# Rotary attention in a six-block decoder: query and content-key projections issued together as paired 64-row matmuls

## What is computed

```python
def _L1_attn_ref(x, W_DQ, W_UQ, W_QR, W_DKV, W_UK, W_UV, W_KR, W_O):
    # D_MODEL 256, N_HEADS 16, D_H 16, D_HR 8, D_LATENT 64; x is the layer-normed stream
    c_q = x @ W_DQ                                        # 64 wide
    Qc = (c_q @ W_UQ) per head;  Qr = rope((c_q @ W_QR) per head)
    c_kv = x @ W_DKV                                      # 64 wide
    Kc = (c_kv @ W_UK) per head; Kr = rope(x @ W_KR), the same for all heads
    V = (c_kv @ W_UV) per head
    scores = clip(concat(Qc, Qr) . concat(Kc, Kr), -80, 80), causal
    weights = softmax(scores / sqrt(24))
    return (weights @ V) @ W_O
x = x + _L1_attn_ref(_layernorm(x), ...)
```

## Time and profile before

| | us |
|---|---|
| median of three runs | 3155.16 |
| lowest, highest | 3151.1, 3158.64 |
| span of the profiled execution | 3229.4 |
| the rotary stage in it, first to last instruction | about 1461.7 to 1735 |
| PE busy in the whole span | 2825.7 (87%) |
| DVE busy | 2269.1 (70%) |
| ACT busy | 1656.0 (51%) |

### The profile page before, as it was taken

One profiled execution on the slowest core, in us unless ns is written; L12 is line 12 of the kernel. 1 busy time (PEld: TensorE's weight loads), 2 busy tenths in 40 slices (PEclk: granted clock), 3 DMA queues, 4 the chain that ended last, 5 costly groups with the idle time before them and its releaser, 6 DMA issues. The chain is left out here.

```text
span 3229.4 us, 75851 instructions
## 1 busy us (share of the span) xinstructions
PE 2825.7 (87%) x28240; PEld 2055.9 (64%) x28240; DVE 2269.1 (70%) x4822; ACT 1656.0 (51%) x3243; POOL 957.9 (30%) x1219
## 2 busy tenths in 40 slices
PE   7998999999999997758997899999997999955880
PEld 6887566666666665547885566666665777745770
DVE  5998567777777775557886677767754999863446
ACT  4776555555655554334553344444444878742330
POOL 0000344555554554440001000000001145445661
PEclk9999999999999998789998899999997999977995
DMA  7930345544555453361000333333314778765557
GB/s 176 292 91 0 113 148 154 159 139 138 162 163 146 138 154 110 115 193 31 0 0 20 65 74 71 72 65 73 73 37 119 219 227 235 219 183 166 171 166 249
DMA packets 364787, 413.71 MB, mean 128 GB/s; under 512 B 108016, under 2 KB 330512, under 8 KB 364368
## 3 DMA queue, kind: packets, MB, share of 16 engines
q1 hardware_dynamic: 218176, 220.63, 25.7%
q10 hardware_dynamic: 127216, 139.94, 15.3%
q0 software_dynamic: 19104, 49.22, 4.5%
HBM read 125.33 MB, written 252.45 MB: 117 GB/s over the span
## 5 line engine op out<-in xcount | busy, mean ns | idle before, releaser
L814 POOL TENSOR_TENSOR x_rstd<-x_var,g_minus_half 112x1 f32<-112x1 f32 x128 | 74.6, 583 | 710.7 <-DVE x_var L810 710.1
L2194 DVE TENSOR_REDUCE x_top<-x_scores 112x2 f32<-112x750 f32 x256 | 228.3, 933 | 81.2 <-PE x_scores L2036 78.7
L1369 ACT ACTIVATE x_probs<-x_held,x_minus_top 112x488 f32<-112x488 f32 x256 | 177.7, 697 | 173.6 <-DVE x_minus_top L1425 173.6
L1242 POOL TENSOR_TENSOR x_probs<-x_probs,x_inverse 112x488 f32<-112x488 f32 x256 | 250.4, 998 | 10.2
L1283 PE MATMUL x_ring<-w_xkv,x_kv 128*122 128x512 f32 x512 | 236.3, 594 | 0.0
L1276 PE MATMUL x_ring<-x_kv,w_xkv 128*128 128x488 f32 x512 | 232.0, 586 | 1.1 <-ACT x_kv L1345 1.1
L932 ACT ACTIVATE x_v<-x_ring 122x512 f32<-122x512 f32 (+1 forms) x224 | 113.0, 505 | 182.9 <-PE x_ring L1283 152.0
L2141 ACT ACTIVATE x_probsT<-x_scores 125x1792 f32<-125x1792 f32 x96 | 159.7, 1664 | 83.3 <-PE x_scores L2056 83.3
L1419 DVE SCALAR_TENSOR_TENSOR x_held<-x_scores,x_keep 112x976 f32<-112x976 f32 x128 | 150.4, 1175 | 73.2 <-PE x_scores L1296 50.8
L814 POOL TENSOR_TENSOR a_rstd<-a_var,g_minus_half 112x1 f32<-112x1 f32 x64 | 35.6, 556 | 537.7 <-DVE a_var L810 537.7
L3102 POOL DMA_INDIRECT expert_replies<-m_rows,m_reply_of x143 | 140.6, 983 | 94.7 <-ACT m_rows L3212 62.3
(11 more groups left out here) (471 smaller groups left out, 7442.7 us busy)
## 6 DMA issues: line engine op xcount, KB each, us to landing
expert_slots<-d_empty ACTq DMA_DIRECT2D x32, 3612.0 KB, 17.3
by_position<-r_by_position SPq DMA_DIRECT2D x64, 784.0 KB
first_slots<-d_empty SPq DMA_DIRECT2D x8, 3612.0 KB, 33.9
r_bias<-by_position SPq DMA_DIRECT2D x64, 392.0 KB
m_rows<-expert_slots SPq DMA_DIRECT2D x143, 129.0 KB
x_kq_swapped<-x_kq_raw ACTq DMA_DIRECT2D x64, 243.5 KB, 3.5
x_slots<-x_kq SPq DMA_DIRECT2D x512, 30.4 KB
m_rows<-expert_replies SPq DMA_DIRECT2D x32, 448.0 KB, 8.5
```

The lines of the kernel that those rows point to most:

```text
L1242: self.nc.gpsimd.tensor_tensor(probs, probs, self.inverse[0:T, u:u + 1].to_broadcast([T, XK]), ALU.mult).then_inc(self.weighted, 1)
L1369: nc.scalar.activation(self.probs[u % 6][0:T, :], self.held[m % 2][0:T, i, :], ACT.Exp, scale=self.scale, bias=self.minus_top[0:T, m % 2, ...
L2194: nc.vector.tensor_reduce(self.top[0:T, g, 2 * half:2 * half + 2], self.scores[0:T, at:at + 1024].rearrange("t (a c) -> t a c", c=512)[:, ...
```

## The change

The steps `q` and `kc` become one piece of PE work. At the place of `q`, PE claims both banks, waits for `a_c`, and then issues eight matmuls in alternation: for each of the four groups one on rows 0 to 63 (`aq` with c_q) and one on rows 64 to 127 (`akc` with c_kv). The halves that were multiplied by zero weights are left out. `kc` keeps its place in the plan for the ring and for DVE, but PE does nothing there. In the plan `q` moves ahead of `turnk`, to right behind `scores`; `kc` moves to behind `scale`, so that DVE makes `a_k` ahead of `bound`; `onT` moves behind `kc`.

```diff
-        self.plan = Flow(4, [("stats", 0), ("scores", 2), ("turnk", 1), ("onT", 4), ("scale", 0), ("q", 1), ("heads", 3),
-                             ("bound", 2), ("kc", 1), ("xT", 0), ("turnq", 1), ("v", 1), ("c", 0), ("kr", 0), ("exp", 2),
+        self.plan = Flow(4, [("stats", 0), ("scores", 2), ("q", 1), ("turnk", 1), ("scale", 0), ("kc", 1), ("onT", 4), ("heads", 3),
+                             ("bound", 2), ("xT", 0), ("turnq", 1), ("v", 1), ("c", 0), ("kr", 0), ("exp", 2),
                              ("project", 4), ("back", 3)])
...
-        elif name in ("q", "kc"):
-            bank = ring.claim(pe, c, body)
-            if name == "q":
-                self.ready(pe, "c", b)
+        elif name == "q":
+
+            spots = {"q": c, "kc": self.plan.order.index("kc")}
+            banks = {n: ring.claim(pe, spot, body) for n, spot in spots.items()}
+            self.ready(pe, "c", b)
             for g in range(HG):
-                ins = nc.tensor.matmul(bank[:, g * T:(g + 1) * T], W["a" + name][:, g * P:(g + 1) * P], self.c[:, :],
-                                       start=True, stop=True)
-            ring.filled(ins, c)
+                for n, rows in (("q", slice(0, 64)), ("kc", slice(64, P))):
+                    ins = nc.tensor.matmul(banks[n][:, g * T:(g + 1) * T], W["a" + n][rows, g * P:(g + 1) * P], self.c[rows, :],
+                                           start=True, stop=True)
+                    if g == HG - 1:
+                        ring.filled(ins, spots[n])
```

## The result

| | before | changed |
|---|---|---|
| median of six runs, us | 3157.85 (3151.1 to 3159.71) | 3181.2 (3167.2 to 3187.24) |
| ratio to before, 95% interval | | 1.0071 (1.0056 to 1.0085) |
| span of the profiled execution, us | 3229.4 | 3180.0 |
| this stage in it, from its first `stats` (808) to the next stage's, us | 1458.66 to 1742.42: 283.8 | 1436.45 to 1746.27: 309.8 |
| frames 4 to 31: start of `a_q_turned`, first to last, us | 1493.2 to 1720.0: 8.40 a frame | 1473.6 to 1723.4: 9.25 a frame |

The account below looks back on a forecast made before the run. A closed chain through PE and DVE was taken to bound the kernel; 18.2 us for 28 full frames plus 2.9 for the end frames gave +21.1, 3155.2 to 3176.3 us, range 3163 to 3200 (own range 3168 to 3187).

Parts of the forecast that it names:

- Which engine bounds the stage: Steady frames: a closed chain through PE and DVE (a_q_turned, project, back, scores, turnk) sets 8.40 us a frame.
- The place: Pair between scores and turnk delays turnk; a full frame grows by X - 0.33 = 0.65 us, to 9.05.
- X: The pair's own time on PE ahead of turnk: 0.88 us plus 0.10 for the pass to full array, 0.98 us.
- slack: Time turnk could come later before DVE's a_kr_plain waits: 0.23 and 0.14 us, mean 0.19 us.
- The wait before a_xn: DVE's wait for the norm's power on POOL, 0.18 us a frame, would give back 0.14 us.
- Their sum: Full frame longer by X - 0.19 - 0.14 = 0.65 us; 18.2 us over 28 frames.
- The frames at the ends: Frames 2, 3 and 32, where DVE already waits for turnk, lose 0.98 us each, 2.9 us; frame 1 loses 0.
- signs of being wrong: Pair under 0.6 or over 1.3 us, a_kr_plain not waiting, project not waiting for a_q_turned, or clock not 1.00.
- PE as the bound: PE's issue time sets each of 32 frames, so its saved time gives -31 us, 3124; chance 0.08.
- The halves not pairing: The 64-row halves of q and kc do not run side by side: X = 1.96, 3206.7 us; chance 0.06.
- X at 0.44: The pair runs at the pace of 32-row tiles: 3159.6 us, no change that shows; chance 0.06.
- The clock falling: PE's clock drops to 0.82 with more idle time: another 21 us over 28 frames, 3197.6 us; chance 0.06.

Follow-up runs that it names:

- run with `turnk` first: Changed kernel with turnk put ahead of the paired q and kc in the plan, against the kernel before: 3156.3 us, ratio 0.9996.
- old order: Paired matmuls with the whole plan of the kernel before, the pair at the place of q, against the kernel before: 3158.47 us, ratio 1.0009.
- freed bank: Changed kernel with turnk ahead of the pair and v ahead of turnq, giving project v's bank, against the kernel before: 3137.0 us, ratio 0.9934.
- line of three kernels: Against the kernel before: changed with half of the pairs behind turnk, 1.0038; changed, 1.0071; changed with full 128-row matmuls, 1.0172.

## Why the prediction was right, point by point

- **Which engine bounds the stage.** Right: a chain closed through both, not PE's 99%. It rests on one reading, that `project` was released by `a_q_turned` with PE's loads idle. The run with `turnk` first shows it directly: PE's loads idle 0.84 us a frame ahead of `project` and nothing is gained (ratio 0.9996). The old order agrees (1.0009), and the freed bank shows the other link, 8.35 to 7.61 us a frame.
- **The place.** Right, and its form too (frame longer by X less the slack): the line of three kernels has slope one. The slack was 0.22 us, 0.19 forecast.
- **X.** Mis-sized: 0.98 forecast, 1.08 measured. The eight pairs take 0.88 us as forecast. The term that was too small is the pass from the pair to the full array: `turnk` loads 1505.53 - 1505.23 = 0.30 us after the last pair where the pace is 0.11, so the pass costs 0.19 or 0.20 us, and 0.10 was forecast. That 0.10 was read in the kernel before from the end of the last load of `scores` to `turnk`. But the loads overlap, and from start to start it is 0.28 us, in the kernel before to `turnk` (1605.24 to 1605.52) and in the changed one to the first pair (1504.17 to 1504.45):

```profile
1504.17 0.17 PEld L1809 LDWEIGHTS a_scores<-a_q,a_k 32*112 32x112 f32 x1
```

  So the way out of `scores` costs the same as before, 0.98 us from its first load, and adds nothing to X; one pass is new, as forecast, with twice its price. By the Trainium skill's rule (TensorEngine Tiling, "Key Properties" under "Tiling Modes": a change of tiling mode drains TensorE) there is a gap at each change of tiling, and the trace agrees with that. The prediction's 1.08 by that rule, a second gap of 0.10, is the measured number by luck.
- **The wait before a_xn.** Wrong by its step "the norm's power on POOL coming late": 0.14 us a frame was to come back and did not. In the changed kernel POOL is done at 1505.30 + 0.55 = 1505.85, DVE's `a_kr_turned` at 1506.66 + 0.28 = 1506.94, and `a_xn` still starts 0.24 us later. In the loop's frames the gap is 0.24 and 0.13 us by turns, 0.18 in the mean, in all nine kernels measured, whatever their order. In frame 2, ahead of the loop, `a_xn` follows after 0.03 us (1452.89 + 0.28 to 1453.20). The trace shows what stands in the gap: register instructions of DVE's own sequencer, which aren't counted as busy. Line 818, where DVE waits for the norm's power ahead of `a_xn`, has one in each of the 28 frames of the loop, and in frames 1 to 3 a plain semaphore wait in its place (DVEq is the sequencer):

```profile
L818 DVEq ALU_OP  x28: 40/40/40, 1470.1 to 1719.9; - x28
```

```profile
L818 DVEq EVENT_SEMAPHORE  x3: 50/50/50, 1444.5 to 1461.2; - x3
```

  In the frame shown it runs at 1507.1, behind another one at 1507.0, both after the end of `a_kr_turned` and ahead of `a_xn` at 1507.17. No run was made without them.
- **Their sum.** +0.85 us a frame instead of +0.65: 0.10 from X, 0.14 from `a_xn`, less 0.03 of slack. Over the 27 frames from the first `a_q_turned` to the last that is 23 us; with the 2.7 and 0.4 us of the next point it makes up the 26.1.
- **The frames at the ends.** Up to `a_q_turned` of frame 4 the stage lost 2.7 us (from the first `stats`: 1493.15 - 1458.66 = 34.5 before, 1473.59 - 1436.45 = 37.1 now). The forecast for this stretch was 2 x 0.98 for frames 2 and 3 and 0.65 for frame 4, 2.6 in all, and that it came out is luck: up to `a_q_turned` of frame 1 it was 0.55 us shorter, and then frames 2, 3 and 4 were 1.72, 0.52 and 0.97 us longer. At the end +1 us was forecast and +0.4 measured (last `a_q_turned` of frame 31 to the next stage, 22.4 and 22.8). Frame 32 did wait 1.75 us for `turnk` where it had waited 0.67, but it grew by only 0.6 us, and the drained frames behind it were 0.2 shorter.
- **The total.** Stage +26.1 in the profile, +22.4 by the ratio of the runs, +21.1 forecast. The range holds them all. The two errors have the same sign and show on the profile's stage, 5 us more than forecast; that the runs came within 1.3 us of the forecast is partly the luck of their spread.
- **What the profile would show.** `a_kr_plain` waits 0.86 us a frame; the prediction's list said 0.5 to 0.7, although its own sum (0.98 less 0.19) gave 0.79. 0.66 before `g_residual` came, 0.97 before `project` came nearly (over a microsecond was forecast). The frame of 9.05 and the end of the wait before `a_xn` did not come. None of the signs of being wrong did.
- **The rivals.** PE as the bound: refuted. The halves not pairing: loads 0.01 us apart, refuted. X at 0.44: 1.08. The clock falling: granted 1.00 in all windows of the stage from 1452 on, with the idle times of 0.3 to 1.0 us in each frame. In the start it did fall once: full in 1444 to 1446, where PE was busy 0.54 of the 2 us, half (0.50) in 1447 to 1449 and full again from 1450. The kernel before had half clock up to 1469, in its frame 1, and full clock from then on. So part of frame 1 ran faster than before and part of frame 2 slower. Only one execution of each kernel is profiled, so whether this belongs to the change isn't shown.

## What to carry to other kernels

When two engines are both nearly always busy, find who released whom at each hand-over and close the loop; time saved outside that loop buys nothing as long as the loop is what sets the pace, and work moved into it costs its full length beyond the slack, which can be read to a tenth of a microsecond before the change. A step that the other engine waits for should be issued ahead of bulk work that nobody waits for yet. In a ring of banks the position in the plan is also a dependency: here a change of two entries that gave `project` another bank, together with the paired matmuls behind `turnk`, made the kernel 0.66% faster where neither alone showed a gain in the runs.

## What the runs showed of the hardware that was not expected

Passes between tilings show in the spacing of the weight loads, best from start to start, since the loads overlap. From the last load of `scores` (32-row tiles) it is 0.28 us to the next step, and the same whether that is the 64-row pair (1504.17 to 1504.45) or `turnk` on the full array (1605.24 to 1605.52). From the last pair (1505.23) to `turnk` on the full array it is 0.30 us, 0.19 more than the usual pace of 0.11. A pair of 64-row fp32 matmuls of 112 columns takes the slot of one full-array matmul, 0.11 us a record. And register instructions of DVE's sequencer stand between two DVE operations in the loop's frames, 0.13 or 0.24 us where the frames ahead of the loop have 0.03.
